# Summing four of fourteen target blocks of a graph layer from gathered rows instead of a dense adjacency product, on one Trainium2 core

## The chip, the cores and the metric

The kernel runs on one core of one Trainium2 chip. The metric is the device time of one execution in microseconds, and the median of the runs is what counts. The engines are called by the names of the profile: PE is TensorE (PEld its weight loads), DVE is VectorE, ACT is ScalarE, POOL is GpSimd, SP is SyncE. A name with a q (SPq, POOLq) is the queue of that engine, where DMAs are issued.

## What is computed

A layer on a graph of 6250 nodes and 106250 directed edges (src, dst, sorted by dst, 17 per node on average). The part that the change touches is the graph part: two ARMA convolutions with K = 2 stacks and T = 3 steps each. In each step a node sums the rows of its sources, scaled by degree factors:

```
for t in range(3):
    h   = einsum(x, init_w) if t == 0 else einsum(out, w)
    h   = segment_sum(h[edge_src] * norm, edge_dst)     # norm = dinv[src] * dinv[dst]
    out = relu(h + root + b)                            # root = einsum(x, root_w)
return out.mean(axis=1)                                 # over the two stacks
```

The first convolution has 128 features per stack (256 in a row of both), the second 64 (128 in a row of both). So there are six sums over edges: three of rows with 256 values, three of rows with 128. Beside them stand a linear attention over x and, at the end, a mixture of six experts over the 6250 nodes; neither is changed.

## The kernel before, in words

The 6250 nodes are padded to 49 tiles of 128 (NP = 6272), which are also 14 windows of 448 columns (WIN, WINS), or 7 pairs of windows (PAIRS).

**The front** (function `front`, first block, up to about 262 us) loads the edges, codes each as dst * 8192 + src, normalizes x, computes keys and values and the root terms, and finds for each group of 8 target nodes where its run of edges starts. A hand-written loop over j = 0 to 87 gives each engine's order: in step j VectorE makes the normed row tile j + 2 (`normed`, L624), and at fixed steps other work is put in: `starts()` at j = 11 (L507 to L514), `column()` at j = 10 to 18, `flags`, `split_codes` and so on behind it. GpSimd fetches runs of 128 edges by indirect DMAs, 14 in L417 and 14 in L422. SP stores the transposed x and the root terms by batches i (L386 to L394), and ACT's `root_out` waits for the stores.

**The build** (`front`, second block, up to about 1014 us) makes the adjacency: for each group of 8 targets DVE writes one-hots (L1092, L1095), PE multiplies them (L1226, L1230) and ACT turns the product into a column stripe of a window, `stage` (L1049), in f16, 49 tiles x 448 columns. SP stores each finished window to `adj_d` (5.5 MB). Between the groups of window w PE already sums window w - 1 for the first step (`passed`, L1241).

**The passes** (function `passes`, a block of its own) are the other five sums, `for t in range(LAST_PASS + 1)` with `BLOCKS = (2, 2, 1, 1, 1)`: t = 0 and 1 are the two-stack passes with 256 values in a row, t = 2 to 4 have 128. In each pass PE goes through 14 windows (`window`, L1515 on). For each of 49 source tiles it multiplies the rows' high and low f16 halves (`part`) with the window's adjacency, which SP loads from `adj_d` in 7 pieces of 7 tiles into one ring (L1417):

```
for r in range(PT):
    h = i * PT + r
    for k in range(BLOCKS[t]):
        for part in range(2):
            m = nc.tensor.matmul(acc[b][k][:, :], src[:, h, part, k * P:(k + 1) * P], ring[:, i, r, :], ...)
```

So a two-stack window has 49 x 4 = 196 matmuls of 448 columns (L1537). When a window's sum is there, DVE scales it, adds the root term and applies relu (L1598 to L1604), PE projects it to the next step's rows (`project`, L1502, L1505, L1507: 3 or 4 tiles in a row, over three banks `pj`; in t = 1 also `r2`, the root term of the second convolution, L1512), and DVE splits them into high and low halves (`rows`, L1580, L1582). The projections of one window are put behind the second piece of the next (`LATER`). All rows stay in SBUF, in `split` or `other` by turns; `fresh_d` is a copy in DRAM of the rows that the first sum has made, and is loaded back (L1033 and, by ACT, L1432).

ACT's queue in the passes holds the loads of `dinv_b` (3136 KB, L1433), of the weights and, in t = 0, 12 stores of zeros to `row_d` (`blank`, L1456, 3340 KB each), and behind them the loads for the last stages. GpSimd has nothing to do from 88 to 2948 us.

**The last stages** (`final`, `experts`, from 2946 us) are the router and the experts; GpSimd scatters rows there by indirect DMAs (L1770, L2250, and L2258 with an accumulation and a bounds check).

What sets the order around the change: SP's list of waits and loads (`column`, L1405 on), PE's hand-written order of pieces and projections, and semaphores that count pieces used (`p_free`), pieces landed (`p_in`), windows finished (`p_hid`) and rows split (`q_lo`).

## Time and profile before

| | |
|---|---|
| median of 3 runs | 3493.51 us (3491.96 to 3496.16) |
| the profiled execution: its span | 3494.5 us; no time beside the span is recorded for it |
| PE busy | 3317.0 us, 95% of the span, 17901 instructions |
| DVE busy | 1260.3 us, 36% |
| ACT busy | 726.4 us, 21% |
| POOL busy | 304.4 us, 9% |
| matmuls of 448 columns in the passes (L1537) | 5488 + 4116 = 9604 |
| pass t = 0 / t = 1 | 1018.65 to 1564.62 / to 2128.69 us |
| passes t = 2, 3, 4 | to 2945.8 us |
| mean DMA rate | 196 GB/s |

The page has a line with 40 slices of the span, each digit the busy share in tenths. Slices 12 to 33 are the passes: PE stands at 9 in each, DVE at 1 or 2, POOL at none. The DMA line has 9 in the first slices of the passes (the zeros are stored there), 4 in the rest of the two-stack passes and 8 or 9 in the single-stack ones. A group's "mean ns" is the time of one instruction from its start to its end; matmuls overlap, so it is not the time from one to the next.

### The profile page before, as it was taken

To read this page: it belongs to the slowest core of one execution; us is meant where nothing else is said; L and a number is where in the kernel's file an instruction comes from. 1 tells how busy PE (TensorE), PEld (TensorE's weight loads), DVE (VectorE), ACT (ScalarE), POOL (GpSimd) and SP (SyncE) were. 2 spreads that over 40 slices of the span, in tenths; PEclk is the share of its full clock that TensorE was granted. 3 is DMA by queue.
4 is the path that set the end of the run, shared out by engine and by line. 5 is a ranking of instruction groups with operands and counts; after the bars stand their busy time and mean duration, and the time that the engine had idled before them with its cause. 6 is when DMAs were issued, how large, how long until landed. Compare 5 with 4: busy or idle time off the path is not lost. (4 is left out here: it accounts for less than half of the span.)

```text
span 3494.5 us, 49444 instructions
## 1 busy us (share of the span) xinstructions
PE 3317.0 (95%) x17901; PEld 1925.9 (55%) x17902; DVE 1260.3 (36%) x4635; ACT 726.4 (21%) x1487; POOL 304.4 (9%) x259
## 2 busy tenths in 40 slices
PE   7998999999989999999999999999999999938998
PEld 4474656566545555555555555555555555625775
DVE  7747777777711111111111111121211002633443
ACT  3445555555500000000000000000000000523333
POOL 3000000000000000000000000000000000364555
PEclk9997999999999999999999999999999999968999
DMA  7212323332389995444444447988889997435886
GB/s 205 66 47 82 145 90 150 156 139 92 154 322 280 321 329 168 157 156 156 143 154 148 149 152 248 322 284 286 286 280 308 304 303 249 153 128 167 199 204 141
DMA packets 220425, 683.53 MB, mean 196 GB/s; under 512 B 26015, under 2 KB 140435, under 8 KB 218242
## 3 DMA queue, kind: packets, MB, share of 16 engines
q1 hardware_dynamic: 156820, 597.56, 50.8%
q10 hardware_dynamic: 41454, 56.62, 5.7%
q0 software_dynamic: 22016, 27.58, 4.1%
q8 instruction: 81, 1.33, 0.2%
q14 instruction: 54, 0.44, 0.0%
HBM read 509.81 MB, written 182.92 MB: 198 GB/s over the span
## 5 line engine op out<-in xcount | busy, mean ns | idle before, releaser
L1537 PE MATMUL acc<-stage,split 128*128 128x448 f16 x5488 | 1045.7, 353 | 4.7 <-PEq L1488 4.7
L1537 PEld LDWEIGHTS acc<-stage,split 128*128 128x128 f16 x5488 | 537.6, 98 | 503.4 <-PEq L1488 4.9
L1537 PE MATMUL acc<-stage,other 128*128 128x448 f16 x4116 | 783.5, 352 | 0.0
L1241 PE MATMUL first_sum<-stage,other 128*128 128x448 f16 x2744 | 648.6, 354 | 0.2 <-ACT stage L1049 0.2
L1537 PEld LDWEIGHTS acc<-stage,other 128*128 128x128 f16 x4116 | 402.8, 98 | 377.0 <-issue 6.0
L1598 DVE TENSOR_TENSOR tmp<-acc,dinv_b 128x448 f32<-128x448 f32 x98 | 61.0, 622 | 1246.9 <-PE acc L1537 1246.9
L1049 ACT ACTIVATE stage<-group_ps 128x392 f16<-128x392 f32 x784 | 385.4, 497 | 295.9 <-PE group_ps L1230 292.6
L1095 DVE TENSOR_SCALAR place<-iota_col,rel 128x196 f16<-128x196 f16 x1568 | 348.8, 265 | 0.0
L1241 PEld LDWEIGHTS first_sum<-stage,other 128*128 128x128 f16 x2744 | 253.7, 98 | 139.1 <-issue 1.3
L1092 DVE TENSOR_TENSOR lanes<-iota_two,lane_two 128x256 f16<-128x256 f16 x784 | 225.1, 287 | 84.5 <-PE group_ps L1230 69.6
L1754 POOL IOTA ids<- 128x49 f32 x1 | 0.2, 172 | 2860.4 <-POOLq L1404 2860.4
L1461 ACT ACTIVATE split<-r,b_two 128x448 f32 x14 | 8.9, 633 | 1115.4 <-PE r L1512 1115.4
L1226 PE MATMUL group_ps<-place,lanes 128*128 128x196 f16 x784 | 199.8, 255 | 31.4 <-DVE place L1095 13.0
L1230 PE MATMUL group_ps<-place,lanes 128*128 128x196 f16 x784 | 200.8, 256 | 0.0
L2258 POOL DMA_INDIRECT out<-slot_out,slot_idx x114 | 176.2, 1545 | 163.6 <-DMA out<-slot_out,slot_idx 97.3
L1867 ACT ACTIVATE dT<-d_ps,params 128x448 f32<-128x448 f32 x14 | 8.9, 633 | 839.5 <-PE d_ps L1785 839.1
L1226 PEld LDWEIGHTS group_ps<-place,lanes 128*128 128x128 f16 x784 | 77.6, 99 | 111.3 <-ACT stage L1049 41.8
L2223 DVE TENSOR_TENSOR slot_out<-out_ps,other 128x256 f32<-128x256 f32 x114 | 48.4, 425 | 186.1 <-PE out_ps L2333 186.1
L1230 PEld LDWEIGHTS group_ps<-place,lanes 128*128 128x128 f16 x784 | 78.0, 100 | 54.3 <-DVE place L1095 0.7
L2317 PE MATMUL one_ps<-other 128*128 128x384 f32 x304 | 105.2, 489 | 0.0
L2333 PE MATMUL out_ps<-other 128*128 128x256 f32 x456 | 104.9, 379 | 0.2 <-ACT other L2278 0.2
L2325 PE MATMUL two_ps<-other 128*128 128x384 f32 x304 | 104.5, 486 | 0.0
(337 smaller groups left out, 2459.6 us busy)
## 6 DMA issues: line engine op xcount, KB each, us to landing
stage<-adj_d SPq DMA_DIRECT2D x490, 784.0 KB, 4.3
adj_d<-stage SPq DMA_DIRECT2D x14, 5488.0 KB, 17.7
row_d<-blank ACTq DMA_DIRECT2D x12, 3340.5 KB, 50.4
other<-pack_d SPq DMA_DIRECT2D x38, 898.0 KB, 4.9
slot_rows<-row_d SPq DMA_DIRECT2D x38, 393.0 KB, 5.4
rin<-root_d SPq DMA_DIRECT2D x28, 448.0 KB, 3.8
xnT_d<-other SPq DMA_DIRECT2D x14, 448.0 KB, 4.2
split<-root_d SPq DMA_DIRECT2D x14, 448.0 KB, 3.9
```

The source lines that it names most:

```text
L1049: nc.scalar.activation(stage[w % 2][:, :, at * G:(at + 1) * G], group_ps[g % BANKS][:, :].rearrange("p (d h) -> p h d", d=G), ACT.Copy).th ...
L1092: nc.vector.tensor_tensor(lanes[:, u % 4, :, :], iota_two[:, :, :], lane_two[:, bass.ds(g, 1), :].broadcast_to([P, P, 2]), ALU.is_equal)
L1095: nc.vector.tensor_scalar(place[:, 2 * u % RING + s, :], iota_col[:, 0:Q4], rel[:, :, :, :].rearrange("p q s g -> p (q s g)")[:, bass.ds(p ...
L1226: mm(group_ps[u % BANKS][:, 0:Q4], lanes[:, u % 4, :, 0], place[:, 2 * u % RING, :], start=True, stop=True, skip_group_check=True)
L1230: return mm(group_ps[u % BANKS][:, Q4:COLS], lanes[:, u % 4, :, 1], place[:, 2 * u % RING + 1, :], start=True, stop=True, skip_group_check ...
L1241: m = mm(acc[b][k][:, 0:WIN], other[:, h, half, k * P:(k + 1) * P], stage[b][:, h, :], start=(h == 0 and half == 0), stop=(h == TILES - 1 ...
L1537: m = nc.tensor.matmul(acc[b][k][:, :], src[:, h, part, k * P:(k + 1) * P], ring[:, i, r, :], start=(h == 0 and part == 0), stop=(h == TIL ...
L1598: v.then(nc.vector.tensor_tensor(one, acc[b][k][:, :], dinv_b[:, bass.ds(w * WIN, WIN)], ALU.mult))
L2258: nc.gpsimd.indirect_dma_start(out[:, :], bass.IndirectOffsetOnAxis(ap=idx[:, b, t:t + 1], axis=0), done[:, b, t, :], None, bounds_check=N ...
L2317: m = mm(one_ps[hc][:, :], weight(b, 0)[:, c, hc * P:(hc + 1) * P], xlT[:, b, c, :], start=(c == 0), stop=(c == 1))
L2325: m = mm(two_ps[hc][:, :], weight(b, 1)[:, c, hc * P:(hc + 1) * P], h1[:, c, :], start=(c == 0), stop=(c == 1))
L2333: m = mm(out_ps[t % 2][:, :], h2[:, c, t * P:(t + 1) * P], weight(b, 2)[:, c, :], start=(c == 0), stop=(c == 1))
```

## The change

Passes t = 0 and t = 1 sum only windows 4 to 13 (`DENSE`, 10 windows) from the adjacency. The targets of windows 0 to 3 are cut into 16 strips of 112 nodes (`UNITS = 4`, `STRIPS = 4`). For each strip 17 runs of 128 edges (a `CHUNK`) are listed, 272 runs in all. For each run GpSimd gathers the 128 source rows (512 f16 values, high and low halves of both stacks) from DRAM with one indirect DMA, DVE writes a one-hot of 128 edges x 112 targets from the edges' keys, and PE multiplies: 4 matmuls of 112 columns. Rows of edges that belong to another strip have no one in the one-hot. The chunks are put between the tiles of the dense windows by a plan, `Course`: the first behind tile 28, the last behind tile 466 of 490. The rows that pass 0 makes are also stored to DRAM (`later_d`), 7 stores, and the gathers of pass 1 wait for all of them.

The lists are made in the front: SP stores the runs' starts and loads them back by 16 small DMAs, DVE computes the runs' rows (`strips_known`, at j = 14), GpSimd makes 4 more gathers, DVE splits the codes (`lists_split`, j = 20), PE transposes them, DVE copies them (`list_kept`, j = 22 and 24). If a strip has more edges than fit its 17 runs, the flag for the long way (`more_edges`) is raised, and all engines take `slow` and `slow_pass`.

Further: build and passes are one block now; the stores of zeros are issued by SP in the build, one behind each of the first 12 windows' stores; `dinv_b` is loaded by ACT behind pass 1 into room that the two-stack passes used, and these passes load the part that they need by window; projections in passes 0 and 1 go one tile at a time, two dense tiles apart, over two banks, high halves on ACT, and the root product of t = 1 goes by tiles of 128 columns; in t = 2 to 4 one projection stands behind each piece. The passes t = 0 and 1 are written out instead of looped. The core of the diff:

```diff
+BLOCKS = (2, 2, 1, 1, 1)
+LAST_PASS = len(BLOCKS) - 1
+UNITS = 4
+STRIP = 112
+STRIPS = WIN // STRIP
+STRIP_GROUPS = STRIP // G
+CHUNK = 17
+LISTED = UNITS * STRIPS * CHUNK
...
+class Course:
+
+    BEGIN, TAIL, LEAD, SETTLE, AFTER, APART = 28, 22, 10, 6, 8, 2
+
+    def __init__(self, windows):
+        self.tiles = windows * TILES
+        self.chunk_at = [self.BEGIN + c * (self.tiles - self.BEGIN - self.TAIL) // LISTED for c in range(LISTED)]
+        self.strip_end = [self.chunk_at[(s + 1) * CHUNK - 1] + 2 for s in range(UNITS * STRIPS)]
+        self.row_at = {}
+        for pair in range(UNITS // 2):
+            for u in range(SUB):
+                self.row_at[(pair, u)] = self.strip_end[pair * 2 * STRIPS + -(-(u + 1) * P // STRIP) - 1] + self.SETTLE
+        for n in range(windows):
+            for place, u in enumerate(TAKEN[n % 2]):
+                self.row_at[((n + UNITS) // 2, u)] = (n + 1) * TILES + self.AFTER + self.APART * place
+        self.row_order = sorted(self.row_at, key=lambda row: (self.row_at[row], row))
+        self.before_end = sum(x < self.tiles for x in self.row_at.values())
+
...
+                    def strips_round():
+                        sp.wait_ge(e_start, 1)
+                        sp.dma_start(strips_d[:, :], start_i[:, :, :].rearrange("g q s -> g (q s)")).then_inc(e_segd, 16)
+                        sp.wait_ge(e_segd, 16)
+                        per = P // 8
+                        for v in range(8):
+                            for n in range(2):
+                                first_group, pair = (v + n) % 8 * STRIP_GROUPS, (v + n) // 8
+                                sp.dma_start(seg_i[v * per:(v + 1) * per, n, :], bass.AP(strips_d.tensor, first_group * 2 * PAIRS + 2 * pair, [[0, per], [2, 2]]),
+                                             allow_slow_non_contiguous=True).then_inc(e_segb, 16)
+
...
+                    pool.wait_ge(e_seg, 2)
+                    for h in range(2):
+                        for q in range(2):
+                            nc.gpsimd.indirect_dma_start(code_s[:, h * 2 + q, :], None, runs_d[:, :],
+                                                         bass.IndirectOffsetOnAxis(ap=run_row[:, h, q:q + 1], axis=0)).then_inc(e_listed, 16)
...
+                    def strips_known():
+                        dve.wait_ge(e_segb, 16 * 16)
+                        e.then(nc.vector.tensor_scalar(seg_i[:, 0, :], seg_i[:, 0, :], 4, None, ALU.logical_shift_right))
+                        e.then(nc.vector.tensor_copy(seg_f[:, :, :], seg_i[:, :, :]))
+                        for h in range(2):
+                            nc.vector.tensor_scalar(run_row[:, h, :], seg_f[:, 0, :], run_add[:, h:h + 1], float(STARTS - 1), ALU.add, ALU.min).then_inc(e_seg, 1)
+                        e.then(nc.vector.scalar_tensor_tensor(over_full[:, :], seg_f[:, 0, :], -float(STEP), seg_f[:, 1, :], ALU.mult, ALU.add))
+                        e.then(nc.vector.tensor_scalar(over_full[:, :], over_full[:, :], CHUNK * P + 0.5, None, ALU.is_gt))
+                        e.then(nc.vector.tensor_tensor(over_full[:, 0:1], over_full[:, 0:1], over_full[:, 1:2], ALU.max))
...
+                    def lists_split():
+                        dve.wait_ge(e_listed, 64)
+                        flat_s = code_s.rearrange("p b e -> p (b e)")
+                        t_s, l_s = (x.rearrange("p b e -> p (b e)").bitcast(I32) for x in (key_s, row_s))
+                        e.done(nc.vector.tensor_scalar(t_s, flat_s, 7, TILE_MASK, ALU.logical_shift_right, ALU.bitwise_and))
+                        e.then(nc.vector.tensor_scalar(l_s, flat_s, P - 1, None, ALU.bitwise_and))
+                        e.done(nc.vector.tensor_copy(l_s.bitcast(F32), l_s))
+                        e.done(nc.vector.tensor_copy(t_s.bitcast(F32), t_s))
+                        e.then(nc.vector.tensor_scalar(flat_s, flat_s, CODE, None, ALU.logical_shift_right))
+                        nc.vector.scalar_tensor_tensor(l_s.bitcast(F32), l_s.bitcast(F32), float(TILES), t_s.bitcast(F32), ALU.mult, ALU.add).then_inc(e_split, 1)
+                        dve.wait_ge(e_split, 1)
+                        for h in range(2):
+                            for q in range(2):
...
+                    if w < CHUNKS:
+                        sp.wait_ge(c_z, 1)
+                        flat = row_d.rearrange("r c -> (r c)").rearrange("(p n f x) -> p n f x", p=P, f=FOLD, x=BLANK)
+                        sp.dma_start(flat[:, w, :, :], blank.unsqueeze(1).broadcast_to([P, FOLD, BLANK])).then_inc(c_blank, 16)
...
+                def stored_at(pair):
+                    at = courses[0].piece_after(courses[0].row_at[(pair, SUB - 1)])
+                    return max(at, (ND - 1) * PIECES) if pair < UNITS // 2 else at
...
+                for t in range(2):
+                    for m in range(ND * PIECES):
+                        n, i = divmod(m, PIECES)
+                        M = t * ND * PIECES + m
+                        if M >= PIECES:
+                            sp.wait_ge(p_free, M - (PIECES - 1))
+                            sp.dma_start(ring[:, i, :, :].rearrange("p t n -> p (t n)"), adj_d[DENSE[n], :, i * PT * WIN:(i + 1) * PT * WIN]).then_inc(p_in[i], 16)
+                        if i == 1:
+                            dense_roots(t, n)
+                        for unit in range(UNITS):
+                            if m == (2 if unit == 0 else courses[t].piece_after(courses[t].strip_end[unit * STRIPS - 1])):
+                                unit_roots(t, unit)
+                        for pair in range(PAIRS):
+                            if M == stored_at(pair):
+                                pair_out(pair)
...
+            @block.gpsimd
+            def _(pool):
+                pool.wait_ge(z_rows, 16 * (PAIRS + 1))
+                pool.wait_ge(b_stored[1], 16 * (PAIRS + 1))
+                pool.wait_ge(s_tab, 2)
+                for t in range(2):
+                    if t == 1:
+                        pool.wait_ge(t_rows, 16 * PAIRS)
+                    for c in range(LISTED):
+                        g = t * LISTED + c
+                        if g >= RING:
+                            pool.wait_ge(s_used, g - (RING - 1))
+                            pool.wait_ge(s_row[g % RING], 16 * (g // RING))
+                        nc.gpsimd.indirect_dma_start(got[:, g % RING, :, :].rearrange("p s c -> p (s c)"), None, tables_d[t].rearrange("p j s c -> (p j) (s c)"),
+                                                     bass.IndirectOffsetOnAxis(ap=tab_row[:, c:c + 1], axis=0)).then_inc(s_row[g % RING], 16)
+                for r in range(RING):
+                    pool.wait_ge(s_row[r], 16 * (2 * LISTED // RING))
...
+                act.wait_ge(p_hid, PASSED)
+                for r in range(RING):
+                    act.wait_ge(s_row[r], 16 * (2 * LISTED // RING))
+                act.dma_start(dinv_b, dinv_d.rearrange("h (o p) -> o (h p)", o=1).broadcast_to([P, NP])).then_inc(b_in, 16)
...
+                def one_hot(t, c):
+                    g = t * LISTED + c
+                    if g == 0:
+                        dve.wait_ge(b_used, WINS * PER + RING // 2)
+                    if g >= HOTS:
+                        dve.wait_ge(s_used, g - (HOTS - 1))
+                    nc.vector.tensor_scalar(hot[:, g % HOTS, :], iota_col[:, 0:STRIP], tab_key[:, c:c + 1], None, ALU.is_equal).then_inc(s_hot, 1)
...
+                def chunk(t, c):
+                    g = t * LISTED + c
+                    s, first = divmod(c, CHUNK)
+                    S = t * PARTED + s
+                    if first == 0 and S >= 2:
+                        pe.wait_ge(s_ev, S - 1)
+                    pe.wait_ge(s_hot, g + 1)
+                    pe.wait_ge(s_row[g % RING], 16 * (g // RING + 1))
+                    for k in range(2):
+                        for part in range(2):
+                            m = mm(group_ps[S % 2][:, k * D:k * D + STRIP], got[:, g % RING, part, k * P:(k + 1) * P], hot[:, g % HOTS, :],
+                                   start=(first == 0 and k == 0 and part == 0), stop=(first == CHUNK - 1 and part == 1), skip_group_check=True)
+                    m.then_inc(s_used, 1)
+
+                def quick_pass(t):
...
+                def quick_pass(t):
+                    course = courses[t]
+                    for x in range(course.tiles):
+                        n, h = divmod(x, TILES)
+                        W, (i, r) = t * ND + n, divmod(h, PT)
+                        if x == 0 and t == 0:
+                            pe.wait_ge(z_back, 16 * (PAIRS - 3))
+                        if x == (PAIRS - 3) * SUB and t == 0:
+                            pe.wait_ge(c_last, 16)
+                        if x == 0 and t == 1:
+                            pe.wait_ge(q_lo, courses[0].before_end)
+                        if x == courses[0].before_end and t == 1:
+                            pe.wait_ge(q_lo, TILES)
+                        if h == 0 and W >= 2:
+                            pe.wait_ge(p_ev, W - 1)
+                        if r == 0:
+                            pe.wait_ge(p_in[i], 16 * (W + 1))
+                        m = tile_sums(t, n % 2, h, i, r)
+                        if r == PT - 1:
+                            m.then_inc(p_free, 1)
+                        for c in course.chunks(x):
+                            chunk(t, c)
+                        if t == 1:
+                            for n, pair, u in courses[0].rows(x + course.tiles):
+                                row_projected(0, n, pair, u)
+                        for n, pair, u in course.rows(x):
+                            row_projected(t, n, pair, u)
...
+                def late_window(t, pair, b, opening):
+                    W = pair * 2 + (PASSED + (t - 2) * WINS + b)
+                    pe.wait_ge(p_ev, W - 1)
+                    for i in range(PIECES):
+                        if opening and b == 0 and i == PIECES - 1:
+                            pe.wait_ge(q_lo, t * TILES)
+                        pe.wait_ge(p_in[i], pair * 32 + 16 * (PASSED + (t - 2) * WINS + b + 1))
+                        for r in range(PT):
+                            m = tile_sums(t, b, i * PT + r, i, r)
+                        m.then_inc(p_free, 1)
+                        if opening and b == 0:
+                            if t == 2 and 1 <= i < 1 + len(TAKEN[1]):
+                                n, last, u = courses[1].rows_left()[i - 1]
+                                row_projected(1, n, last, u)
+                            elif t > 2:
+                                late_projected(t - 1, PAIRS - 1, 1, i - 1)
+                        elif t < LAST_PASS:
+                            late_projected(t, pair - 1 if b == 0 else pair, 1 - b, i - 1)
...
-                        pe.wait_ge(q_lo, pair * SUB + (t * TILES + u + (PJ if u == 0 else 1)))
...
```

## Rows read from the trace of the kernel before

**Rows 1.** Windows: busy us of PE, PEld, DVE, ACT, POOL (instructions), clock, DMA share, GB/s.
```profile
80.00:100.00 20.00, 15.36 (x67) 7.84 (x66) 19.18 (x46) 7.53 (x16) 5.99 (x7) 0.97 0.18 55
...
160.00:180.00 20.00, 20.00 (x102) 11.05 (x100) 10.41 (x30) 10.61 (x23) 0.00 (x0) 1.00 0.14 46
...
1500.00:1600.00 100.00, 99.54 (x538) 53.07 (x537) 14.93 (x32) 0.00 (x0) 0.00 (x0) 1.00 0.47 150
```
**Rows 2.** Timeline: first matmuls of passes t=0, t=1, t=2: start, length, engine, line.
```profile
1018.65 1.65 PE L1537 MATMUL acc<-stage,split 128*128 128x448 f16 x4 [4.75 <-PEq L1488]
...
1564.62 10.57 PE L1537 MATMUL acc<-stage,other 128*128 128x448 f16 x55
...
2128.69 5.46 PE L1537 MATMUL acc<-stage,split 128*128 128x448 f16 x28
```
**Rows 3.** Instruction groups by line, TensorE: count, busy us, mean ns, idle before, releaser.
```profile
L1537 PE MATMUL acc<-stage,split 128*128 128x448 f16 x5488 | 1045.7, 353 | 4.7 <-PEq L1488 4.7
...
L1507 PE MATMUL pj<-w_two,hid 128*128 128x128 f32 x196 | 30.1, 282 | 9.1 <-DVE other L1582 4.5 <-DVE split L1582 4.5
...
L1502 PE MATMUL pj<-w_one,hid 128*128 128x128 f32 x196 | 26.0, 278 | 3.2 <-DVE other L1582 3.2
L1505 PE MATMUL pj<-w_two,hid 128*128 128x128 f32 x196 | 26.0, 278 | 1.5 <-DVE split L1582 1.5
...
L1512 PE MATMUL r<-hid,w_rtwo 128*128 128x448 f32 x56 | 23.4, 540 | 0.0
```
**Rows 4.** Timeline, TensorE: a 196-column matmul and its successor; matmuls of 6 columns.
```profile
500.11 0.25 PE L1230 MATMUL group_ps<-place,lanes 128*128 128x196 f16 x1
500.20 0.35 PE L1241 MATMUL first_sum<-stage,other 128*128 128x448 f16 x1
...
3000.94 0.17 PE L1838 MATMUL rank_ps<-chosen,above 128*128 128x6 f16 x1
...
3001.27 0.17 PE L1839 MATMUL rank_ps<-chosen,g_ones 128*128 128x6 f16 x1
```
**Rows 5.** Timeline, GpSimd: a gather, a long scatter, a scatter of the last stage.
```profile
86.88 0.93 POOL L422 DMA_INDIRECT split<-runs_d,start  x1 [0.31 <-issue]
...
3019.22 1.94 POOL L1770 DMA_INDIRECT row_d<-rows,seat_idx  x1 [0.30 <-issue]
...
3177.93 1.57 POOL L2258 DMA_INDIRECT out<-slot_out,slot_idx  x1 [0.30 <-issue]
```
**Rows 6.** DMA issues with median us to landing, and a queue's share, 3074 to 3110.
```profile
fresh_d<-split SPq DMA_DIRECT2D x7, 896.0 KB, 5.7
...
dinv_b<-dinv_d ACTq DMA_DIRECT2D x1, 3136.0 KB, 20.9
...
split<-runs_d,start POOLq DMA_INDIRECT x14, 2.6
...
bounds_d<-bound_i SPq DMA_DIRECT2D x1, 3.1 KB, 15.1
...
q0 software_dynamic: 1344, 3.76, 30.1%
```
**Rows 7.** Instruction groups by line, VectorE: columns as in rows 3.
```profile
L1095 DVE TENSOR_SCALAR place<-iota_col,rel 128x196 f16<-128x196 f16 x1568 | 348.8, 265 | 0.0
...
L549 DVE SCALAR_TENSOR_TENSOR below<-below 112x1792 f32<-112x1792 f32 x1 | 2.0, 2026 | 0.0
```
**Rows 8.** Windows at the start of pass t=0, columns as in rows 1.
```profile
1018.00:1022.00 4.00, 3.35 (x10) 1.35 (x11) 0.51 (x2) 0.00 (x0) 0.00 (x0) 0.50 0.60 188
1022.00:1026.00 4.00, 4.00 (x18) 1.88 (x17) 0.00 (x0) 0.00 (x0) 0.00 (x0) 0.79 1.05 387
```
**Rows 9.** Timeline of the front: SP's issue of two small loads, VectorE at j=11 and j=14.
```profile
32.88 1.18 SPq L363 DMA_DIRECT2D b_one<-in_L_gnn_b  x2
...
69.81 0.17 DVE L512 TENSOR_SCALAR start<-start_i 112x14 uint32<-112x14 uint32 x1
...
81.25 0.69 DVE L628 TENSOR_REDUCE ss<-sq 128x8 f32<-128x512 f32 x1
```

737 lines of the change are left out of this document (481 added, 256 removed).

## The prediction

> **What bounds the kernel now.** I read the windows first. In the stretch where the second stage sums a two-stack pass, TensorE (the first number after the length) is busy 99.54 of 100 us at full clock, while VectorE has 15, ScalarE and GpSimd nothing, and the DMA engines are taken to 0.47 [rows 1]. So a matmul that leaves these passes leaves the span, and whatever joins them on TensorE lengthens it. Two other windows show the front: at 80 to 100 us VectorE is the busy one (19.18 of 20) and TensorE waits for it (15.36 of 20); at 160 to 180 us it is the reverse, TensorE 20 of 20. Work or waits added to VectorE before about 140 us are therefore paid in full, later ones not.
>
> **Term 1, the dense windows removed.** The three starts in [rows 2] bound the two passes: t=0 runs from 1018.65 to 1564.62 (546.0 us), t=1 to 2128.69 (564.1 us). Pass t=0 holds 14 x 49 x 4 = 2744 matmuls of 448 columns and its projections, 26.0 us busy and 3.2 us of waiting [rows 3]. (546.0 - 29.2) / 2744 = 0.188 us each; the group's mean of 353 ns is the latency of one, not its turn. Four windows are 784 matmuls: 147.4 us a pass, **-294.8 us**.
>
> **Term 2, the chunks added.** A pass gets 272 chunks of 4 matmuls, each 112 columns with new weights: 1088. No such row exists. Below lie the f16 matmuls of 6 columns with 128x128 weights: 13 starts between 3000.94 and 3001.27, 0.025 us each [rows 4]. So loading weights does not hold up more than that. Above lies the 196-column matmul, whose successor starts 0.09 us later [rows 4]. On the line between them 112 columns is 0.025 + 106/190 x 0.065 = 0.061; but a streaming matmul's turn follows its columns (448 take 0.188, so 112 take 0.047), and I take 0.050. That is 54.4 us a pass, **+108.8 us** (from 54 to 196 by the two ends).
>
> **GpSimd's turn, costed at nothing.** Each chunk needs one indirect transfer of 128 rows of 1 KB. The gathers of now cost 0.93 us plus 0.31 before it, a turn of 1.24 [rows 5]. TensorE's own turn per chunk is longer: 440 tiles for 272 chunks is 1.62 tiles of 4 x 0.188, 1.22 us, plus 0.20 for the chunk and 0.10 as its share of projections: 1.51 us. The cover is thus only 0.27 us a turn. A gather lands 2.6 us after its issue [rows 6], and a ring of 8 gives it some 10 us. The queue row says 30.1% of 16 engines for 36 us of scatters, which come every 1.27 us: 6.1 us of engine time each [rows 6]; 272 of them are 23% of a 449 us pass, beside some 41% for the thinner dense loads. No bound. VectorE's one-hot is at most the 0.265 us of the 196-wide one [rows 7], 72 us a pass, hidden.
>
> **Term 3, the start of pass 0.** The end of a block goes: 4.75 us in which TensorE waited [rows 2], and the slow start behind it, clock 0.50 and then 0.79 [rows 8], the lower level and half-way back: 3.35 x 0.5 + 4 x 0.21 = 2.5 us. **-7.2 us**. The loads that pass 0 needs are issued as before, and tile 28 is 21 us away.
>
> **Term 4, the start of pass 1.** Gathers of pass 1 read rows that pass 0 has just made, and wait for all seven stores. SP issues the last store only behind the piece that waits for 74 pieces used, which is tile 28 of pass 1. TensorE reaches it at 21.1 + 2.1 (four projections) = 23.2 us; the store lands 5.7 us later [rows 6], the gather 2.6 and about 1 of start-up after that: 32.5 us. Behind SP's wait stands nothing urgent, for the ring of pieces is full; behind GpSimd's stand all gathers. TensorE, in order, stands at chunk 0: 9 us, plus 2.5 for the clock as in term 3. **+11.5 us** (0 if the store were out earlier, 17 if it lands under load). The gap does not grow later, 1.24 being under 1.51.
>
> **Term 5, the start of pass 2.** dinv_b, 3136 KB, moves from the covered start of pass 0 to behind pass 1: ScalarE issues it after the four last rows, whose products stand behind pieces 1 to 4, some 18 us into pass 2. Before, it landed in 20.9 us [rows 6], with a 2.7 MB load ahead of it; I take 15. VectorE waits for it, queued behind is the finish of window 0, and TensorE asks for that at the first row of window 1, 28 us into the pass; it gets it at 18 + 15 + 2 = 35 to 36: 8 us, and 2.5 of clock. **+10.5 us** (0 to 17).
>
> **Term 6, projections spread out.** Four in a row over three banks waited for VectorE: 3.2, 1.5 and 9.1 us [rows 3]. One per piece, or two tiles apart, has no such wait: **-13.8 us**. The r product of 56 matmul records, 23.4 us, becomes 196 of 128 columns at 26.0/196 [rows 3]: **+2.6 us**.
>
> **Term 7, the front.** The strip table goes out when starts are known, 70.0 us [rows 9]. A tiny DMA issued at 57 took 15.1 us to land amid the x loads [rows 6]; at 70 I take 10, landing at 80. Then SP issues 16 small DMAs at 0.59 each as b_one's pair shows (1.18 for two) [rows 9], but some rows of this kind are shorter, so 8 to 9 us, and 2 to land: 90 or 91. VectorE reaches strips_known at 81.2 [rows 9] and waits 9 us with every normed row, and so TensorE, queued behind it. SP's stores of batch 1 stand behind too, needed only at j=17. Then its own work: 8 small steps of 0.17, six over 512 columns at no more than 2026 x 512/1792 = 0.58 us [rows 7], eight small ones: 6 us. Four more gathers on GpSimd, 5 us, end before j=20. **+15 us** (4 to 28).
>
> The blank stores, 12 of 3.3 MB, move to SP's queue in the build, behind each window's store; what they could hold up is the next root load, a whole window away. Nothing.
>
> **Sum.** -294.8 + 108.8 - 7.2 + 11.5 + 10.5 - 13.8 + 2.6 + 15.0 = -167.4. From the profiled execution's 3494.5 us: 3327.1; that execution stands 1.0 above the median of the runs, so 3326.
>
> **Rivals.**
> A. GpSimd's turn is the longer one. The scatters of the last stage take 1.57 + 0.30 [rows 5]. For: the cover is 0.27 us. Against: those have a bounds check and an accumulation, these have not. Pass 0: 21.1 + 264 x 1.87 + 16.5 (22 tiles) = 531 for 449; pass 1: 33 + 271 x 1.87 + 16.5 = 556 for 486. +152: 3478 us. What might lengthen the turn is VectorE. The Trainium skill's page "SBUF — State Buffer", section "Who interferes with whom", says that a VectorE instruction in a two-port mode and GpSimd fully block each other and that tensor_scalar can enter such a mode. By that rule each turn could grow by one one-hot, to 1.24 + 0.27 = 1.51, level with TensorE, and the time be 3326 to 3347; the short turns among busy VectorE stretches so far speak against more.
> B. The small matmuls do not hide their loads and take the 0.083 us of 196 columns rather than 0.050: 2176 x 0.033 = +72: 3398 us. The 6-column rows speak against.
> C. **Slower.** Single turns of 1.94 + 0.30 stand among the others [rows 5]. If this is the usual turn, with the DMA queues loaded throughout as they are not in the stretches seen, pass 0 is 21.1 + 264 x 2.24 + 16.5 = 629 and pass 1 is 656.5: +350, 3676 us. It decides from a turn of 1.90 us: A's 1.87 leaves 15 us of gain, and each 0.1 us costs 54. Only about one turn in seven is so long in the row's neighbourhood.
> D. It does not run. A strip of over 2176 edges raises the flag for the long way. A strip has 112 x 17 = 1904 on average, so I hold it unlikely; the long way would give back the 186 of terms 1 and 2 and lose the build's overlap with 2744 x 0.188 = 516 us: 4028 us.
> E. The three waits of terms 4, 5 and 7 do not show: -11.5 - 10.5 - 15: 3289 us.
>
> **Numbers.** Forecast 0.57, E 0.12, B 0.13, A 0.11, C 0.05, D 0.02. A range from 3280 to 3410 takes in forecast, E and B with the ends of the unknown terms, 0.82. A change of 0.2% (7 us) is what a measurement can tell: faster 0.91, within it 0.02 (A's edge), slower 0.07.
>
> **What would show it.** The acc group has 9604 - 1568 = 8036 matmuls, a new group of 2176 with 112 columns takes 100 to 125 us busy, and GpSimd has 544 more transfers with starts 1.5 us apart, as TensorE sets them. In pass 1 TensorE waits some 9 us at tile 28 for a gather, in pass 2 some 8 us before the first product of window 1, in the front VectorE some 9 us near 81 us. It is wrong if, in the passes, TensorE waits regularly for gathers with transfers 1.8 us apart or more, or if pass 0 takes over 500 us.

## The result, and the profile after

The changed kernel takes 3316.9 us (median of four runs, 3315.5 to 3317.4) against 3494.6 for the kernel before in runs beside it: ratio 0.9494, with a 95% interval of 0.948 to 0.9507. The forecast was 3326 and its range 3280 to 3410, so time and sign were right. The profiled execution spans 3315.3 us, 179.2 less than the one of before; the forecast sum was -167.4.

The page's groups of the changed kernel (line, engine, operation, out<-in, count, then busy time, mean ns of one, and the idle time ahead):

```profile
L1831 PE MATMUL first_sum<-stage,split 128*128 128x448 f16 x4704 | 949.7, 354 | 1.9 <-DMA split<-fresh_d 1.9
L1831 PE MATMUL first_sum<-stage,other 128*128 128x448 f16 x3332 | 687.2, 353 | 0.0
L1308 POOL DMA_INDIRECT stage<-fresh_d,lane_two x272 | 261.5, 961 | 1088.1 <-DMA fresh_d<-split 933.4
L1308 POOL DMA_INDIRECT stage<-later_d,lane_two x272 | 261.6, 962 | 217.7 <-PE group_ps L1873 122.5
L1873 PE MATMUL group_ps<-place,stage 128*128 128x112 f16 x2176 | 196.3, 213 | 9.9 <-DMA stage<-later_d,lane_two 9.9
L1580 DVE TENSOR_SCALAR place<-iota_col,lane_two 128x112 f16<-128x112 f16 x544 | 110.0, 255 | 147.5 <-PE group_ps L1873 146.6
```

The counts are those announced: 4704 + 3332 = 8036 dense matmuls in the passes, 2176 small ones, 544 gathers. The small matmuls show 9.9 us of idle time ahead of them in all, from one wait. GpSimd waits for TensorE, not the other way. The 196.3 us of "busy" is not the 100 to 125 that I announced: a group's busy time takes in the tails that overlap the next matmuls, so it was the wrong place to look for a price. The starts have it.

One window in the middle of pass 0, with the columns of [rows 1]:

```profile
1300.00:1400.00 100.00, 100.00 (x745) 61.39 (x743) 29.32 (x105) 7.11 (x15) 62.67 (x66) 1.00 0.74 249
```

TensorE is as full as before, at full clock. VectorE has 29 us for 15, GpSimd 63 for none, and the DMA engines have gone from 0.47 to 0.74: they carry fewer dense pieces per us and the gathers on top.

Where passes begin, and TensorE's waits there (start, us, [idle before <- releaser]), to be laid beside [rows 2]:

```profile
1016.74 1.51 PE L1793 MATMUL pj<-split 128*128 128x128 f32 x8 [3.43 <-DVE split L1484]
...
1022.50 0.93 PE L1831 MATMUL first_sum<-stage,split 128*128 128x448 f16 x2 [1.89 <-DMA split<-fresh_d]
...
1471.34 1.49 PE L1831 MATMUL first_sum<-stage,other 128*128 128x448 f16 x7
...
1505.16 0.53 PE L1873 MATMUL group_ps<-place,stage 128*128 128x112 f16 x4 [9.94 <-DMA stage<-later_d,lane_two]
...
1951.58 1.68 PE L1831 MATMUL first_sum<-stage,split 128*128 128x448 f16 x8
...
1985.90 0.80 PE L1957 MATMUL pj<-stage 128*128 128x128 f32 x2 [6.75 <-DVE stage L1662]
...
2233.74 1.49 PE L1831 MATMUL first_sum<-stage,other 128*128 128x448 f16 x7
...
2504.09 1.11 PE L1831 MATMUL first_sum<-stage,split 128*128 128x448 f16 x5
...
2767.09 1.37 PE L2206 MATMUL d_ps<-other,rel 128*128 128x448 f32 x3 [2.41 <-PEq L1199]
```

Both announced waits stand at their places: 9.94 us at tile 28 of pass 1 (9 forecast) and 6.75 us ahead of the first product of window 1 in pass 2 (8 forecast). From these starts comes the account, in us:

| stretch | before | after | change | forecast |
|---|---|---|---|---|
| to the start of pass 0 | 1018.65 | 1022.50 | +3.9 | +10.3 |
| pass 0 | 546.0 | 448.8 | -97.1 | -98.7 |
| pass 1 | 564.1 | 480.2 | -83.8 | -80.4 |
| passes 2 to 4 | 819.5 | 815.5 | -4.0 | +1.4 |
| last stages | 546.3 | 548.2 | +1.9 | 0 |
| sum | 3494.5 | 3315.3 | -179.2 | -167.4 |

(The forecast column is the eight terms put where they act: 15 - 4.75 at the start; -147.4 + 54.4 - 3.2 - 2.5 in pass 0; -147.4 + 54.4 + 11.5 - 1.5 + 2.6 in pass 1; 10.5 - 9.1 later.)

The front: SyncE's strip round, VectorE's wait for it, and TensorE's first matmul behind the front, in the changed kernel and, in the last line, before:

```profile
69.89 0.32 SPq L433 DMA_DIRECT2D strips_d<-start_i  x1
74.37 7.32 SPq L439 DMA_DIRECT2D seg_i<-strips_d  x16
...
83.16 0.17 DVE L569 TENSOR_SCALAR seg_i<-seg_i 128x2 uint32<-128x2 uint32 x1 [2.07 <-DMA seg_i<-strips_d]
...
278.80 0.32 PE L1766 MATMUL group_ps<-place,lanes 128*128 128x196 f16 x1 [10.38 <-issue]
```

```profile
271.57 0.32 PE L1226 MATMUL group_ps<-place,lanes 128*128 128x196 f16 x1 [10.42 <-issue]
```

SyncE could go on 4.5 us after it began to issue the table, where I had 10 for its landing, and the 16 small loads took 7.3 us to issue. VectorE waited 2.07 us, not 9. TensorE's last work of the front, by the idle time in the last two lines, now ends at 268.4 us instead of 261.15, so 7.3 later.

GpSimd at the start of pass 1:

```profile
1502.26 0.95 POOL L1308 DMA_INDIRECT stage<-later_d,lane_two  x1 [59.30 <-DMA later_d<-other]
1503.52 0.95 POOL L1308 DMA_INDIRECT stage<-later_d,lane_two  x1 [0.30 <-issue]
```

Its turn is 0.95 + 0.30 = 1.256 us, as [rows 5] had it. Over both passes its gathers start 1.50 us (pass 0) and 1.56 us (pass 1) apart, counted from the ninth gather of a pass on as all mean turns below, as TensorE sets them. It looked as if the sum was right for the reasons given. What the rows don't say is how near the other side was, and that is what the experiments were for.

### The profile page after: what moved, and what is told of

Read it like the earlier page. It is cut to its first block and busy times, and to the rows that moved or that the text cites. A ratio compares the mean times of both kernels' runs of the same rounds, so it can differ in the third digit from the quotient of the medians.

```text
span 3315.3 us, 51940 instructions
## 1 busy us (share of the span) xinstructions
PE 3133.6 (95%) x18657; PEld 1902.1 (57%) x18658; DVE 1341.3 (40%) x5159; ACT 771.9 (23%) x1620; POOL 834.1 (25%) x808
## 5 line engine op out<-in xcount | busy, mean ns | idle before, releaser
L1831 PE MATMUL first_sum<-stage,split 128*128 128x448 f16 x4704 | 949.7, 354 | 1.9 <-DMA split<-fresh_d 1.9
L1831 PE MATMUL first_sum<-stage,other 128*128 128x448 f16 x3332 | 687.2, 353 | 0.0
L1831 PEld LDWEIGHTS first_sum<-stage,split 128*128 128x128 f16 x4704 | 450.1, 98 | 374.3 <-issue 5.3
L1781 PE MATMUL first_sum<-stage,other 128*128 128x448 f16 x2744 | 648.9, 354 | 0.2 <-ACT stage L1323 0.2
L1308 POOL DMA_INDIRECT stage<-fresh_d,lane_two x272 | 261.5, 961 | 1088.1 <-DMA fresh_d<-split 933.4
L1831 PEld LDWEIGHTS first_sum<-stage,other 128*128 128x128 f16 x3332 | 315.1, 98 | 244.7 <-issue 1.4
L1781 PEld LDWEIGHTS first_sum<-stage,other 128*128 128x128 f16 x2744 | 253.7, 98 | 139.4 <-issue 2.0
L1308 POOL DMA_INDIRECT stage<-later_d,lane_two x272 | 261.6, 962 | 217.7 <-PE group_ps L1873 122.5
L1873 PEld LDWEIGHTS group_ps<-place,stage 128*128 128x128 f16 x2176 | 160.1, 98 | 110.0 <-issue 10.8
L1873 PE MATMUL group_ps<-place,stage 128*128 128x112 f16 x2176 | 196.3, 213 | 9.9 <-DMA stage<-later_d,lane_two 9.9
L1580 DVE TENSOR_SCALAR place<-iota_col,lane_two 128x112 f16<-128x112 f16 x544 | 110.0, 255 | 147.5 <-PE group_ps L1873 146.6
L1766 PEld LDWEIGHTS group_ps<-place,lanes 128*128 128x128 f16 x784 | 77.6, 99 | 111.4 <-ACT stage L1323 41.6
```

The lines of the kernel that those rows point to most:

```text
L1308: nc.gpsimd.indirect_dma_start(got[:, g % RING, :, :].rearrange("p s c -> p (s c)"), None, tables_d[t].rearrange("p j s c -> (p j) (s c)") ...
L1580: nc.vector.tensor_scalar(hot[:, g % HOTS, :], iota_col[:, 0:STRIP], tab_key[:, c:c + 1], None, ALU.is_equal).then_inc(s_hot, 1)
L1766: mm(group_ps[u % BANKS][:, 0:Q4], lanes[:, u % 4, :, 0], place[:, 2 * u % RING, :], start=True, stop=True, skip_group_check=True)
L1781: m = mm(acc[b][k][:, 0:WIN], other[:, h, half, k * P:(k + 1) * P], stage[b][:, h, :], start=(h == 0 and half == 0), stop=(h == TILES - 1 ...
L1831: m = mm(acc[b][k][:, 0:WIN], side(t)[:, h, part, k * P:(k + 1) * P], ring[:, i, r, :], start=(h == 0 and part == 0), stop=(h == TILES - 1 ...
L1873: m = mm(group_ps[S % 2][:, k * D:k * D + STRIP], got[:, g % RING, part, k * P:(k + 1) * P], hot[:, g % HOTS, :], start=(first == 0 and k ...
```

## The experiments

Beside each time stands the ratio to the kernel before on the same chip. The record numbers the chips: e1 to e4 ran on chip 14, e5, e6, e7 and f5 on chip 11, e8, f6 and f7 on chip 3, e9 on chip 2; for the changed kernel it gives no number. By the time of the kernel before they are of two kinds, and it matters. On chips 11 and 2 it took 3493 and 3498 us, and 3494.6 beside the changed kernel: I call these the faster kind. On chips 14 and 3 it took 3533 and 3534: the slower kind. Pass lengths, from the first dense matmul of a pass to that of the next, are compared beside the ratios: the third and the fourth pass (t = 3 and 4) take 270.4 and 263.0 us on both kinds, while e1's last stages are 27.7 us longer than those of the changed kernel. What differs in the passes comes to light with e4. Two stretches that the edits leave as they are show the scatter: on the faster kind, pass 0 starts at 1018.25 (e7) to 1023.77 us (e9) in the five kernels with the same front, and the last stages take 545.1 (f5) to 549.7 us (e6).

**e1: without the gathers.**

```diff
-                    for c in range(LISTED):
+                    for c in range(RING if t == 0 else 0):
...
-                    pe.wait_ge(s_row[g % RING], 16 * (g // RING + 1))
+                    pe.wait_ge(s_row[g % RING], 16)
```

> Only the first 8 of the 544 row gathers are issued, all in pass 0; every chunk multiplies what lies in its ring slot. The rows of windows 0 to 3 are thus not the reference's. If GpSimd's turn is covered, as I hold, only the one wait for a gather at the start of pass 1 goes (9.9 us, and about 1 us of slow clock behind it): 3306 us. If the gathers cost more than that wait, through their DMA traffic beside the dense pieces or through VectorE, whose one-hots run beside them, it is under 3295 us.

Measured: ratio 0.9457 (0.943 to 0.9483), 0.0037 or 13 us under the changed kernel; the intervals just touch, and the starts of the passes say it more sharply. Pass 0 took 448.7 us for 448.8, pass 1 468.2 for 480.2. So pass 0 is not changed by 264 gathers fewer, and pass 1 gets shorter by 12.0 us: the wait of 9.94, and 2.1 that I put down to the slow clock behind it (granted 0.50 from 1500 to 1508 us in the changed kernel). Costing the gathers at nothing beside that wait was right for this kernel.

**e2: twice as many gathers for the same bytes.**

```diff
-                        nc.gpsimd.indirect_dma_start(got[:, g % RING, :, :]..., ap=tab_row[:, c:c + 1] ...).then_inc(s_row[g % RING], 16)
+                        for part in range(2):
+                            nc.gpsimd.indirect_dma_start(got[:, g % RING, part, :], ..., element_offset=part * D).then_inc(s_row[g % RING], 16)
```

(The waits on `s_row` count 32 where they counted 16.)

> Each gather of 128 rows of 1 KB is made by two of 128 rows of 512 bytes: the bytes are the same, GpSimd's instructions doubled. If GpSimd's turn is 0.95 + 0.30 us per instruction whatever the bytes, a chunk takes 2.51 us and GpSimd sets the pace: pass 0 is 21 + 264 x 2.51 + 16.5 = 700 us for 448.8, pass 1 34 + 271 x 2.51 + 16.5 = 731 for 480.2: +502, 3819 us. If the turn goes by bytes, a chunk stays near 1.26 us and the time at 3317; with only the 0.30 doubled it is 1.56, level with TensorE's turn, 3317 to 3350.

Measured: 4085 us, ratio 1.1559 (1.154 to 1.1579); pass 0 819.5 us, pass 1 844.6. GpSimd did become the bound, and its price goes by the instruction: 955 ns each for half the bytes. But I had expected 700 and 731 us; both passes are 114 to 120 us longer than instructions of 1.256 us make them, and the starts of the gathers are 1.456 us apart in pass 0 on average. What lies between them comes with e4.

**e3: half of the small matmuls.**

```diff
-                        for part in range(2):
+                        for part in range(1):
                             m = mm(group_ps[S % 2][:, k * D:k * D + STRIP], got[:, g % RING, part, k * P:(k + 1) * P], hot[:, g % HOTS, :],
```

> Of the 4 matmuls of a chunk only the 2 of the high halves are made, so the rows of windows 0 to 3 miss the low halves: 1088 matmuls fewer over both passes. At the 0.050 us of the prediction: -54, 3263 us. At the 0.083 of rival B: -90, 3227. At the 0.025 of the 6-column rows: -27, 3290. GpSimd's turn of 1.26 us stays under TensorE's of about 1.4.

Measured: ratio 0.9426 (0.9411 to 0.9442), some 24 us under the changed kernel's ratio; pass 0 440.9 us, pass 1 468.2. Pass 0 alone would say (448.8 - 440.9) / 544 = 0.015 us for a small matmul, less than any of the three prices. It says something else, as e8 shows.

**e4: the chunks closer together.**

```diff
-    BEGIN, TAIL, LEAD, SETTLE, AFTER, APART = 28, 22, 10, 6, 8, 2
+    BEGIN, TAIL, LEAD, SETTLE, AFTER, APART = 28, 190, 10, 6, 8, 2
```

> The plan's TAIL goes from 22 to 190 tiles: the same 272 chunks stand one behind each tile, so TensorE's turn between two chunks falls to 0.75 + 0.19 = 0.94 us and what projections add, under GpSimd's 1.256. If that turn is fixed, TensorE waits at every chunk: pass 0 is 21 + 264 x 1.256 + 190 x 0.752 + about 5 for rows = 501 us for 448.8, pass 1 34 + 271 x 1.256 + 143 + 5 = 522 for 480.2: +94, 3411 us. If GpSimd can go faster where it is asked to, or the cover does not matter, it stays at 3317.

Measured: ratio 1.0145 (1.0128 to 1.0162), so some 1.5% slower than the kernel before; pass 0 569.0 us, pass 1 595.4, where I expected 501 and 522. GpSimd in the middle of its pass 0:

```profile
1103.06 0.95 POOL L1308 DMA_INDIRECT stage<-fresh_d,lane_two  x1 [0.30 <-issue]
1104.32 0.95 POOL L1308 DMA_INDIRECT stage<-fresh_d,lane_two  x1 [0.30 <-issue]
1106.65 0.95 POOL L1308 DMA_INDIRECT stage<-fresh_d,lane_two  x1 [1.38 <-DMA split<-runs_d,start]
1107.90 0.95 POOL L1308 DMA_INDIRECT stage<-fresh_d,lane_two  x1 [0.30 <-issue]
```

Each instruction has its 1.256 us, but mostly every fourth to seventh one waits another 0.9 to 1.5 us, and the mean of pass 0 is 1.477. The releaser that the row names, a load of the front, is a mistake of the inference; what stands ahead of a gather are two waits for its slot in the ring, that the gather of eight turns ago has landed and that TensorE has used it. Neither held this one. TensorE's last four matmuls on that slot were these:

```profile
1100.77 0.36 PE L1873 MATMUL group_ps<-place,stage 128*128 128x112 f16 x4
```

They end at 1101.13 us, and GpSimd ends its previous gather at 1105.27 and then stands for 1.38 us. So it is throughout: of 94 idle stretches of over 0.8 us ahead of e4's gathers (both passes, without their starts), 93 begin when the slot has already been used, 85 of them over 2 us later; they hold 111 us beyond the usual 0.30. In e2 it is 108 of 109 and 196 us. In the changed kernel it is 3 of 78. TensorE waits too (the waits of TensorE: total, times, longest):

```profile
PE group_ps L1873 <- issue: 55.8, 90, 2.8
...
PE first_sum L1831 <- issue: 38.7, 70, 1.1
PE group_ps L1873 <- DMA stage<-later_d,lane_two: 26.0, 15, 9.8
PE group_ps L1873 <- DMA stage<-fresh_d,lane_two: 25.1, 23, 3.5
```

My theory at this point was: gathers land late now and then, later than a ring of 8 can bear; the rival: the queues can't carry more. On it rest the expectations of e6, e5 and e9. Both overlook that GpSimd's slots were free, and the larger half of these rows, the waits that end in "issue". One of them, in TensorE's order:

```profile
1111.07 0.35 PE L1831 MATMUL first_sum<-stage,split 128*128 128x448 f16 x1
1112.32 0.73 PE L1831 MATMUL first_sum<-stage,split 128*128 128x448 f16 x3 [0.90 <-issue]
1113.75 0.36 PE L1873 MATMUL group_ps<-place,stage 128*128 128x112 f16 x4 [0.70 <-issue]
```

TensorE stops between the first and the second of the four matmuls of one dense tile, where the code has no wait at all. No late gather can do that.

**e6: e4 with a ring of 12.** `GR = 12` takes the place of `RING` in every wait and slot of the gathers; ten blocks lie where eight lay, two in a tile that only the long way uses.

```diff
+        GR = 12
...
-                        if g >= RING:
-                            pool.wait_ge(s_used, g - (RING - 1))
-                            pool.wait_ge(s_row[g % RING], 16 * (g // RING))
+                        if g >= GR:
+                            pool.wait_ge(s_used, g - (GR - 1))
+                            pool.wait_ge(s_row[g % GR], 16 * (g // GR))
```

> The close chunks of e4 (one behind each tile) with a ring of 12 gathered blocks for 8. e4 came out at 1.0145 of before, 3545 us on the scale of 3494.6, with a turn of 1.48 us a chunk where I expected 1.256. If that comes from gathers that land late now and then, later than a ring of 8 can bear, 12 blocks bring the turn back to near 1.28: 544 x 0.20 = 109 us less, 3436 us, ratio 0.983. If it is the rate at which the queues move the gathers' packets, nothing changes: 3545 us, 1.0145.

Measured: ratio 0.9806 (0.9791 to 0.9821), 3426.8 us; pass 0 506.8, pass 1 534.9. This is nearly the time that I expected, and yet not the proof that I wanted, for it ran on a chip of the faster kind and e4 on one of the slower, and no pause of the kind "issue" stands in its passes. TensorE's idle time in pass 0 and pass 1, summed from its rows by kernel, chip and kind of wait (without the wait at the very start of pass 0):

| kernel | kernel before on its chip | gathers | "issue" | other |
|---|---|---|---|---|
| changed, f5, e7, e5, e6, e9 | 3493 to 3498 | 544 | 0 in each | for gathers; in e7 also for banks, in e5 and e9 0.6 and 0.5 for one-hots |
| e1, e8 | 3533 | 8 | 0 | 0 |
| f6 / f7 | 3533 | 544 | 7.2 / 6.8 | 0 |
| e3 | 3533 | 544 | 13.9 | 21.1 |
| e4 | 3533 | 544 | 110.2 | 58.2 |
| e2 | 3533 | 1088 | 414.8 | 18.2 |

Part of "issue" stands at instructions that do have a wait in the code, and there a wait whose end the trace lacks can hide in it (7.2 of e3's, 29 of e4's, 57 of e2's); the rest can't be a wait. So the pauses are seen only where two things meet: a chip of the slower kind, and gathers. In e4 and e2, where GpSimd is at its limit, they are by far the most. No kernel but the one before was run on both kinds, and it has no trace from the slower. The part that the chip plays is thus read from this table, not from one kernel run on both. What e6 shows by itself is that the queues carry a gather every 1.26 us beside the dense pieces: the rival falls. The ring is hardly what it was: past the start of pass 0 no gather of e6 is used later than 9.8 us after its start, within the 10.0 that eight turns give. Of the 62 us that e4 takes more in pass 0, the idle stretches of GpSimd with a free slot are 52, so most of it is the chip and not the ring.

One guess at the cause, instructions that reach the engine late, can be held against the DMA rows. The queue that loads instructions has the same row in pass 0 of e4 and of e6:

```profile
q8 instruction: 27, 0.44, 0.3%
```

With 27 loads against 87 pauses on TensorE in that pass, and no greater share of the DMA engines than where there is no pause, nothing here speaks for it; the cause stays open.

**e5: the changed kernel with a ring of 4.** The same edit with `GR = 4` and the plan of the changed kernel.

> The changed kernel with a ring of 4 gathered blocks for 8. TensorE's turn of 1.5 us gives a gather 4 x 1.5 = 6 us from its issue to its use; 0.95 for the issue and the median landing of 4.0 fit in. If landings were all near 4 us it stays within 5 us of 3317. If many land later, as e4 suggests, TensorE waits for them: over 3360 us.

Measured: ratio 0.9724 (0.9702 to 0.9745), 3396.4 us; pass 0 487.7, pass 1 521.4. TensorE's waits (total, times, longest):

```profile
PE group_ps L1881 <- DMA stage<-later_d,lane_two: 36.1, 23, 10.0
PE group_ps L1881 <- DMA stage<-fresh_d,lane_two: 26.9, 27, 3.4
```

Fifty waits where the changed kernel has one, on a chip of the same kind. The changed kernel's landings, in the view of the gathers' line (duration in ns min/median/max), are the other half:

```profile
L1308 POOL DMA_INDIRECT stage<-fresh_d,lane_two x272: 947/952/1363, 1026.8 to 1442.0; - x136
L1308 POOL DMA_INDIRECT stage<-later_d,lane_two x272: 947/952/1387, 1502.3 to 1921.4; - x136
...
DMA to landing us min/median/max: 2.6/4.0/8.7
```

A gather lands 4.0 us after its issue in the middle and 8.7 at the worst (the trace has the landing of one in eight, 68, and 10 of these are at 6.0 us or above). A ring of 8 at TensorE's pace gives it some 11 us (past the start of pass 0, gathers are used 9.0 to 13.2 us after their start), a ring of 4 some 6. Here the theory of late gathers holds: 6 us are too short, 11 are enough. And here GpSimd does wait for its slots: all 131 of its idle stretches of over 0.8 us begin before the slot has been used.

**e9: e4 without the dense pieces' loads.** This asks what makes them late.

```diff
                         if M >= PIECES:
                             sp.wait_ge(p_free, M - (PIECES - 1))
-                            sp.dma_start(ring[:, i, :, :]..., adj_d[DENSE[n], :, ...]).then_inc(p_in[i], 16)
...
-                            pe.wait_ge(p_in[i], 16 * (W + 1))
+                            pe.wait_ge(p_in[i], 16)
```

> The close chunks of e4 with its ring of 8, and the pieces of the adjacency are loaded once, at the start, for both two-stack passes, instead of 140 times: the sums of windows 5 to 13 are not the reference's, and the gathers have the DMA engines nearly for themselves. e4's pass 0 was 569.0 us, with a ring of 12 it was 506.8, and a turn of 1.256 throughout gives 504. If the late gathers of e4 come from the 784 KB pieces ahead of them, pass 0 is 504 to 508 here with the ring of 8; pass 1 34 + 271 x 1.256 + 143 + 5 = 522 to 535. If they come from the gathers themselves (descriptors, DRAM, VectorE), it stays near 569 and 595.

Measured: ratio 0.981 (0.9793 to 0.9826), 3428.5 us; pass 0 510.3, pass 1 530.9, with the ring of 8. One window of e4, e6 and e9, in this order, with the columns of [rows 1]:

```profile
1060.00:1370.00 310.00, 239.09 (x1786) 137.89 (x1784) 84.75 (x302) 11.27 (x24) 202.95 (x210) 0.97 0.59 191
```

```profile
1060.00:1370.00 310.00, 267.40 (x2104) 161.83 (x2102) 102.40 (x349) 13.80 (x30) 235.08 (x246) 0.96 0.68 222
```

```profile
1060.00:1370.00 310.00, 270.08 (x2096) 153.72 (x2094) 99.97 (x351) 13.75 (x29) 235.16 (x246) 0.99 0.43 129
```

GpSimd issues 210 gathers in the 310 us of e4 and 246 in e6 and e9, one each 1.26 us, its limit. Without the pieces a ring of 8 reaches that too. The expectation was nearly met (510.3 for 504 to 508), but again against e4 from a chip of the other kind, whose trace has no landing of a gather at all, so that the pieces made e4's gathers late is not shown. What chips of the faster kind show: the median landing is 2.8 us in e9, 3.5 in e6 and 4.0 in the changed kernel. So gathers land 0.7 to 1.2 us later beside the pieces (ring and pace differ too), and even without them a single one takes 9.3. The Trainium skill's page "DMA: Bandwidth & Descriptors", section "Queues, rings and completion order", has an engine take turns between its queues by whole packets, which agrees with a gather being slower beside other loads; how long a packet of the pieces holds one up, no run here shows.

**e8: e1 and e3 together**, for the price that e3 could not show (the edits of both).

> e1 and e3 together: 8 gathers in all and only the 2 high matmuls of each chunk, so that nothing can wait for a gather and the price of a small matmul stands alone; the rows of windows 0 to 3 are not the reference's. Against e1's pass 0 of 448.7 us, 544 matmuls fewer: at the 0.050 us of the prediction 421.5 us, at the 0.083 of rival B 403.5, at 0.025 435. If e3's 440.9 us was held up by gathers, as I hold now, it is the first: 421 to 423, and the whole 52 us under e1.

Measured: ratio 0.929 (0.9276 to 0.9304); pass 0 422.0 us, pass 1 441.4. Against e1, on a chip of the same kind and like it without a pause: 26.7 us for 544 matmuls in pass 0 and 26.8 in pass 1, **0.049 us each**. e3's pass 0 of 440.9 us is 18.9 longer with the same matmuls, and beside the chip (14 for 3, both of the slower kind) the gathers are the only difference: pauses and waits of 14.4 us stand in it, of which only 1.2 bear the name of a gather.

**e7: the projections in a row again.**

```diff
-    BEGIN, TAIL, LEAD, SETTLE, AFTER, APART = 28, 22, 10, 6, 8, 2
+    BEGIN, TAIL, LEAD, SETTLE, AFTER, APART = 28, 22, 10, 6, 8, 0
```

> APART from 2 tiles to 0: the 3 or 4 projections of a dense window stand in a row again, over two banks. If the spread is what took the 13.8 us of waits away (term 6), they come back, and more of them with two banks for three: +10 to +20 us, 3327 to 3337. If VectorE and ScalarE are quick enough for two banks in any case, 3317 to 3320.

Measured: ratio 0.9515 (0.95 to 0.9529), 3323.2 us, by the ratios 7 us above the changed kernel: between the two ranges that I had. The intervals overlap, but the trace has it by place:

```profile
PE pj L1845 <- DVE other L1587: 7.3, 10, 0.7
...
PE group_ps L1873 <- DMA stage<-later_d,lane_two: 6.2, 1, 6.2
...
PE pj L1847 <- DVE split L1587: 2.7, 9, 0.3
```

10.0 us of waits for banks come back, which the changed kernel has not at all, and 3.7 us of the first wait for a gather go, since the last rows of pass 0 and so their store are earlier. Pass 0 takes 456.0 us for 448.8 and pass 1 481.9 for 480.2; that pass 0 also starts 4.3 us earlier is the scatter named above, for the edit changes nothing ahead of it.

**f5: three moves against the three new waits.**

```diff
-                    return max(at, (ND - 1) * PIECES) if pair < UNITS // 2 else at
+                    return max(at, (ND - 1) * PIECES) if pair < UNITS // 2 else at - 2 * (pair == PAIRS - 1)
...
+                act.dma_start(dinv_b, ...).then_inc(b_in, 16)
                 for n, pair, u in courses[1].rows_left():
                     row_high(1, n, pair, u)
-                act.wait_ge(p_hid, PASSED)
...
-                        if j == RUN_AT + 5:
+                        if j == RUN_AT + 7:
                             strips_known()
```

(The waits ahead of dinv_b's load move with it.)

> Three moves in one kernel, each with its own place in the trace. The last store of pass 0's rows is issued two pieces (14 tiles, 10.5 us) earlier in SyncE's list: it lands some 21.5 us into pass 1, the first gather 2.9 later at 24.4, TensorE asks at 23.3: the wait of 9.94 falls to 1 to 2 us and the slow clock behind it goes. dinv_b is loaded ahead of the four last rows' scaling by ScalarE, some 12 us earlier: the wait of 6.75 us in pass 2 goes, and about 1.5 of slow clock. strips_known two steps later: VectorE's 2.07 us of waiting go. Together -9 -8 -2: 3298 us, ratio 0.944. If these waits are only passed on (the gathers then meet the loads of pass 1's start, dinv_b the dense pieces), 3310 or more.

Measured: 3299.4 us, ratio 0.9444 (0.9431 to 0.9457). VectorE's wait in the front is gone and the front ends 0.9 us earlier; that pass 0 starts 1.4 us earlier is within the scatter. Pass 1 takes 474.5 us for 480.2, pass 2 273.0 for 282.2. The first two chunks of pass 1 and the first products of window 1 in pass 2:

```profile
1494.54 0.36 PE L1873 MATMUL group_ps<-place,stage 128*128 128x112 f16 x4 [0.83 <-DMA stage<-later_d,lane_two]
1494.73 0.92 PE L1831 MATMUL first_sum<-stage,other 128*128 128x448 f16 x4
1497.87 0.53 PE L1873 MATMUL group_ps<-place,stage 128*128 128x112 f16 x4 [2.21 <-DMA stage<-later_d,lane_two]
```

```profile
1971.70 0.38 PE L1957 MATMUL pj<-stage 128*128 128x128 f32 x2
```

3.0 us are left of the 9.94, in two waits (I had 1 to 2), and of the 6.75 nothing.

**f6: f5, chunks of pass 1 from tile 34, ring of 12.**

```diff
-        courses = [Course(ND), Course(ND)]
+        courses = [Course(ND), Course(ND, 34)]
```

> f5 with two more moves: in pass 1 the chunks begin behind tile 34 instead of 28, and the ring has 12 gathered blocks. f5's pass 1 was 474.5 us with 3.0 us of waits for the first gathers and a slow clock behind them; e1's, which had no gather, 468.2. If those waits are all that is left of the gathers' price, pass 1 comes to 469 +- 1 and the whole to 3294. If the tighter turn (1.49 us) brings the late gathers of e3 into play, ring or no ring, pass 1 stays at 474 or more.

Measured: ratio 0.9442 (0.943 to 0.9455), the same as f5, on a chip of the slower kind. A miss: pass 1 took 476.3 us, not 469. No wait for a gather is left in it, but at 1507 to 1515 us stand the pauses:

```profile
1508.65 0.54 PE L1839 MATMUL first_sum<-stage,other 128*128 128x448 f16 x2 [1.21 <-issue]
...
1511.46 0.53 PE L1839 MATMUL first_sum<-stage,other 128*128 128x448 f16 x1 [1.75 <-issue]
```

Single dense matmuls come one by one, and from 1512 to 1516 us the DMA share is 0.12 and the granted clock 0.50, the lower level. The pauses of pass 1 are 5.4 us and the slow clock comes on top, about what it is too long by. Whether f6 is at 469 on a chip of the faster kind was not tried.

**f7: f6, and the rows ahead of the pieces.** SyncE issues two of the seven pieces of the adjacency, then the four loads of rows, then five pieces.

> f6, and SyncE issues the four loads of rows for pass 0 behind the second of the seven adjacency pieces instead of behind all. f5 waited 2.18 us for these loads with the DMA engines full. Pass 0 starts about 2 us earlier and the whole is 3292. If the pieces or the last load of rows are then late instead, the 2 us come back inside pass 0, and it stays at f6's time.

Measured: ratio 0.9424 (0.9411 to 0.9437), the lowest of the kernels that leave nothing out, though its interval overlaps those of f5 and f6. Pass 0 begins with no wait for rows, 4.2 us after the first of the last projections instead of 6.3, and takes 449.0 us for f6's 450.4. So within these two stretches the 2 us stayed won, though the absolute start of pass 0 (1022.7 us for 1022.5) lies within the scatter. f7 is 0.7% under the changed kernel and 5.8% under the kernel before, by ratios to the kernel before on each one's chip.

## Why the prediction was right, and where it was not

**Term 1** was exact in kind: the starts of passes before divided by their matmuls gave 0.188 us, and pass 0 came out within 1.6 us of its sum.

**Term 2**, the point with the widest bounds (54 to 196 us), was right: 0.049 us by e8 for the 0.050 taken. The choice of a streaming matmul's columns over the line between the 6-column and the 196-column row was what made it so; rival B's 0.083, with 1088 such matmuls in a pass, would have put pass 0 at 485. Only my check for it was at fault, as said above.

**GpSimd at nothing** held. The turn is 1.256 us for the 1.24 that [rows 5] gave, TensorE's 1.50 for 1.51, and e1 finds no price beside the first wait. Two things in the step were too simple. I took a landing of 2.6 us from the front; under load it is 4.0 in the middle and 8.7 at the worst, and a mean DMA share, by which I judged it, doesn't show that. The ring of 8 bears it, one of 4 costs 80 us (e5). And I took the turn of the instruction for the limit of the stream. On the faster kind of chip it is (e6, e9). On the slower the mean turns came to 1.477 us in e4 and 1.456 in e2, by idle stretches of GpSimd ahead of free slots, which no row of before shows, so there the cover of 0.27 us is nearly used up: e3, at a turn of some 1.41 us for TensorE, already loses 19 us of pass 0.

**Rivals A and C** share the mechanism that shows in e2: GpSimd's stream as the bound of the passes. At two turns a chunk both passes together took 735 us more than the changed kernel's, and the kernel was 15.6% slower than the one of before. The point from which that rival decides, 1.90 us, lies between the 1.50 of the changed kernel and e2's 2.91 a chunk. The gather instruction itself hardly moved: 952 ns in the middle, and 20 of the 544 took 1.02 to 1.39 us. All 20 overlap one of VectorE's single-input f32 steps that finish a window or a strip (L1557, L1559, L1572); none that meets only one-hots or no VectorE work at all took over 1 us. And VectorE's tensor_scalar instructions stretch beside gathers. First the one-hots and the window step of the changed kernel, then the same of e1, which has 8 gathers (duration in ns min/median/max):

```profile
L1580 DVE TENSOR_SCALAR place<-iota_col,lane_two x544: 129/246/475, 1021.7 to 1923.2; 128x112 f16<-128x112 f16 x182
...
L1557 DVE TENSOR_SCALAR stage<-stage x20: 379/426/584, 1067.0 to 1953.9; 128x448 f32<-128x448 f32 x20
```

```profile
L1580 DVE TENSOR_SCALAR place<-iota_col,lane_two x544: 128/244/253, 1025.8 to 1915.4; 128x112 f16<-128x112 f16 x182
...
L1557 DVE TENSOR_SCALAR stage<-stage x20: 382/385/388, 1071.3 to 1946.1; 128x448 f32<-128x448 f32 x20
```

The Trainium skill's rule that VectorE in a two-port mode and GpSimd block each other (page "SBUF — State Buffer", section "Who interferes with whom") agrees with this: where they meet, one or the other takes longer. (e3, on e1's own chip and with all its gathers, has one-hots of up to 502 ns.) But it did not make a gather longer by a one-hot each, as rival A had feared, only the mean gather by 9 ns.

**Term 3** was half right. The wait of 4.75 us fell to 1.89, now for the loads of rows. The slow start did not go, since TensorE had been idle before it in any case, for VectorE at the last window (3.43 us):

```profile
1022.00:1026.00 4.00, 3.50 (x10) 1.50 (x11) 0.46 (x3) 0.00 (x0) 0.00 (x0) 0.50 0.84 278
1026.00:1030.00 4.00, 4.00 (x19) 1.84 (x17) 0.00 (x0) 0.00 (x0) 2.63 (x3) 0.80 0.71 220
```

The granted clock is 0.50, the lower level, and then 0.80, as in [rows 8]. Here taking a wait away did not give the clock back, as another idle stretch stood ahead of it. In f7, which took the rest of the wait, the slow stretch lies mostly under the last projections, and the granted clock is 1.00 again from 1024.5 us, 1.8 us into pass 0.

**Term 4**: 11.5 us forecast, 12.0 by e1. Right, with its mechanism: f5's earlier store took 5.7 us of pass 1 away. The closeness is in part luck: the last later_d store landed in 7.1 us rather than 5.7, while GpSimd's start-up took 0.3 us rather than 1.

**Term 5**: 10.5 forecast (8 of wait and 2.5 of clock), 6.75 of wait measured and 9.1 us by f5 with what follows. Right; dinv_b landed in 14.7 us for the 15 assumed.

**Term 6**: -13.8. e7 puts 10.0 us of waits back in passes 0 and 1, where [rows 3] have only 3.2 + 1.5, because two banks are shorter than three. In passes 2 to 4, the change of -4.0 with f5's 9.1 for dinv_b leaves -13.1 for what the spread and the rest of the rewriting did, where I had -9.1. The waits of before that are gone there are 9.2 us; where the other 4 come from, no run shows. The direction is right, the size in the late passes is not.

**Term 7** was the mis-sized one: +15 forecast, +7.3 measured at the end of the front. The wait was 2.07 us for 9, since the tiny table held SyncE for 4.5 us and not 10: I had leaned on the 15.1 us of a transfer issued 13 us earlier, in the midst of the x loads. VectorE's own work was the rest, some 5 us for 6. f5 moved the wait away, and its front ends 0.9 us earlier. The end of the front is the firmer measure here: with the same front it is 268.2 to 269.9 us on the faster kind of chip, while the start of pass 0 scatters over 5.5 us.

The last stages took 1.9 us longer, but the same code there took 545.1 to 549.7 us in the runs on the faster kind of chip, so this is no effect of the change that could be told from scatter.

Summed up, the miss of 11.8 us is 6.4 at the start (term 7, less term 3; a good part of it can be scatter), 5.4 in the late passes (term 6) and 3.4 in pass 1, less 1.6 in pass 0 and 1.9 at the end.

## What to carry to other kernels

A stream that one engine issues and another uses through a ring has two limits: the turn of its instruction, and the slots of its ring over the time from issue to landing; the second goes by the latest landings under the load of that stage, not by the mean share of the DMA engines. Which of the two holds it is read from one comparison, whether the slot had been used when the issuing engine fell idle; in e5 it had not, in e4 it had, and a larger ring can't help there. Price an instruction by taking it away only where nothing else is about to hold the engine up: e3 gave 0.015 us for what costs 0.049. And before two kernels are compared across chips, find out from a stretch with the same code how far it scatters, and sort the idle time of both by what ended it: idle time that only one kind of chip has, at places where the code has no wait, belongs to neither kernel's design.

## What the runs showed of the hardware that was not expected

- An indirect gather of 128 rows costs GpSimd 0.95 + 0.30 us whether the rows have 1 KB or 512 bytes (955 ns on average in e2, 961 and 962 in the changed kernel).
- Its landing goes from a median of 2.8 us without loads of 784 KB (e9) to 3.5 and 4.0 beside them (e6, changed kernel), at mean DMA shares of 0.43, 0.68 and 0.74.
- VectorE's tensor_scalar instructions and GpSimd's gathers stretch each other: f16 one-hots of 128x112 take up to 475 ns beside gathers for 253 without, f32 steps of 128x448 up to 584 for 388, and 20 of 544 gathers 1.02 to 1.39 us for 0.95. The tensor_tensor steps beside them (L1553) stay at 616 ns for 614 in the middle.
- A 112-column f16 matmul with weights of its own costs 0.049 us in a full stream, as its share of columns says (112/448 of 0.188 is 0.047), so its weight load is hidden.
- On two chips of the slower kind (14 and 3) TensorE pauses between matmuls that have no wait between them, by up to 2 us (e2), in every kernel with all its gathers, and never in those with 8 gathers in all (e1, e8); 14 us of the passes in e3, 415 in e2. GpSimd stands idle ahead of free slots there too, 111 us in e4. On the faster kind no such pause of TensorE is seen, and of GpSimd at most 3 such stretches a kernel. The cause is open.
